# Context mean and residual input moved between the steps of a linear-attention layer

## The reference

```
x = layernorm(x + L0_attn(x))          # linear attention, 16 heads of 16
x = layernorm(x + L0_xattn(x, ctx))    # x @ W1.T + mean(ctx) @ W2.T + b
x = layernorm(x + L0_ffn(x))           # mixture of experts
```

## Time and profile before

| what | value |
|---|---|
| median of 3 runs | 2200.93 us (2196.56 to 2201.04) |
| the profiled execution | 2198.03 us, of which 2195.9 us lie between its first and last instruction |
| mean granted PE clock | 0.955 of full speed |
| PE busy, DVE busy over the span | 1986.5 us (90%), 1532.8 us (70%) |
| the attention of layer 0 | from the start to about 329 us |

### The profile page before, as it was taken

The page is one execution under the profiler, slowest core; times in us unless marked ns, Lnnn a source line. Parts: engine busy times, 40 slices in busy tenths (PEclk is TensorE's granted clock), DMA queues, the critical chain, the costliest instruction groups (busy, mean ns, idle before and its releaser), DMA issues. The chain is left out here.

```text
span 2195.9 us, 36045 instructions
## 1 busy us (share of the span) xinstructions
PE 1986.5 (90%) x12788; PEld 1413.2 (64%) x12788; DVE 1532.8 (70%) x2463; ACT 1152.0 (52%) x2215; POOL 964.9 (44%) x752
## 2 busy tenths in 40 slices
PE   7898876997988885899999999999999996799997
PEld 4565555995553553566666666666666663799996
DVE  5777764545878988588898988888888886222223
ACT  3332311110277455688877887678876772233333
POOL 2233232222322241077666666667666674222223
PEclk9999997998899997999999999999999997899998
DMA  4100007413000000200100010000000001621113
GB/s 162 40 23 23 24 16 276 171 40 113 0 0 1 1 30 0 69 1 1 31 1 1 1 40 2 1 1 1 11 1 1 1 11 68 263 74 39 36 36 127
DMA packets 37158, 95.63 MB, mean 44 GB/s; under 512 B 5492, under 2 KB 24696, under 8 KB 32248
## 3 DMA queue, kind: packets, MB, share of 16 engines
q1 hardware_dynamic: 31032, 77.07, 9.7%
q0 software_dynamic: 5952, 16.26, 2.3%
HBM read 78.89 MB, written 14.42 MB: 42 GB/s over the span
## 5 line engine op out<-in xcount | busy, mean ns | idle before, releaser
L2232 POOL TENSOR_TENSOR x_total<-x_total,x_pt 128x1024 f32<-128x1024 f32 x189 | 446.9, 2364 | 152.2 <-ACT x_pt L2318 133.5
L2341 ACT ACTIVATE x_pt<-PS,x_maskf 128x512 f32<-128x512 f32 x544 | 333.2, 689 | 125.0 <-PE PS L2677 121.3
L2445 DVE TENSOR_TENSOR PS<-x_pt,PS 128x512 f32<-128x512 f32 x480 | 333.5, 695 | 48.0 <-ACT x_pt L2341 10.5
L2463 DVE TENSOR_TENSOR x_pt<-x_pt,PS 128x1024 f32<-128x1024 f32 x320 | 323.2, 1053 | 0.7 <-PE PS L2695 0.7
L2677 PE MATMUL PS<-x_qs,x_ks 64*128 64x256 f32 x2176 | 287.9, 396 | 1.2 <-ACT x_pt L2341 1.0
L2318 ACT ACTIVATE x_pt<-x_pt 128x1536 f32<-128x1536 f32 (+1 forms) x160 | 264.1, 1664 | 13.7 <-DVE x_pt L2463 13.4
L2654 PE MATMUL PS<-x_pt,x_vs 128*64 128x256 f32 x2108 | 262.8, 388 | 2.0 <-issue 1.8
L2677 PEld LDWEIGHTS PS<-x_qs,x_ks 64*128 64x128 f32 x2176 | 195.5, 187 | 81.5 <-issue 60.1
L1163 PEld LDWEIGHTS PS<-m_xT,m_own 128*128 128x128 f32 x1984 | 236.0, 196 | 8.2 <-DVE m_own L1243 2.9
L1163 PE MATMUL PS<-m_xT,m_own 128*128 128x128 f32 x1984 | 236.9, 279 | 4.1 <-DVE m_own L1243 2.4
L1175 PE MATMUL PS<-f_w,m_hT 128*128 x992 | 224.1, 379 | 0.0
(11 more groups left out here) (321 smaller groups left out, 2914.6 us busy)
## 6 DMA issues: line engine op xcount, KB each, us to landing
f_w<-in_L_ffn_w SPq DMA_DIRECT2D x32, 1024.0 KB, 6.3
a_ctxT<-in_ctxT SPq DMA_DIRECT2D x8, 800.5 KB, 4.2
l_w<-in_ctx SPq DMA_DIRECT2D x4, 1024.0 KB
f_w<-ys SPq DMA_DIRECT2D x16, 256.0 KB, 5.2
l_w<-in_L_attn_w SPq DMA_DIRECT2D x6, 512.0 KB, 6.6
a_xT<-in_xT SPq DMA_DIRECT2D x4, 512.0 KB, 5.8
X<-in_x SPq DMA_DIRECT2D x1, 2048.0 KB, 11.2
xr<-a_xn SPq DMA_DIRECT2D x16, 128.0 KB, 1.7
```

The source lines that it names most:

```text
L2232: ins = nc.gpsimd.tensor_tensor(total2[:], first, tile[:, 2 * k + 2:2 * k + 4, :], ALU.add)
L2341: nc.scalar.activation(pt[:, s % 2, t, :].rearrange("p (h n) -> p h n", h=2), PS[:, first:first + 2, half], ACT.Identity, bias=maskf[:, b ...
L2445: ins = nc.vector.tensor_tensor(acc, tile, acc, ALU.max)
L2463: nc.vector.tensor_tensor(p_, p_, PS[:, MB, None, :].to_broadcast([P, at.stop - at.start, SPAN]), ALU.subtract).then_inc(lowered, 1)
```

## The change

- `mean(b, 0)` of batches 1 to 3 moves from place 0 of step s = 2 to the end of the step before it (1, 5, 9). `mean(b, 1)` moves from place 0 of step s = 3 to the end of the first step of the batch itself (4, 8, 12).
- The product with W2 and `context` move from the end of step s = 3 to place 1 of step s = 1 of the batch itself (1, 5, 9, 13), behind the second round of scores, and the order of the uses of the shared PSUM bank changes with them.
- `residual_input` is made for one tile in each of steps 0 to 15 (128 x 256) instead of for four tiles at once.

```diff
-            for kind, t in (("logits", g_ - 4), ("x1", g_ - 3), ("o", g_ - 2)):
+            if tile(g_ - 4):
+                OUT_USE["logits", g_ - 4] = len(OUT_USE)
+            if tile(g_) and g_ % J == 1:
+                OUT_USE["context", g_ // J] = len(OUT_USE)
+            for kind, t in (("x1", g_ - 3), ("o", g_ - 2)):
                 if tile(t):
                     OUT_USE[kind, t] = len(OUT_USE)
-            if g_ % J == J - 1 and g_ // J + 1 < B:
-                OUT_USE["context", g_ // J + 1] = len(OUT_USE)
...
-            def residual_input(b):
+            def residual_input(t):
                 pool.wait_ge(w_loaded, 16 * 7)
                 pool.wait_ge(x_loaded, 16)
-                x = X[:, b * J:(b + 1) * J, :]
-                nc.gpsimd.tensor_tensor(x, x, bout[:, None, :].to_broadcast([P, J, D]), ALU.add).then_inc(xres_ready, 1)
+                nc.gpsimd.tensor_tensor(X[:, t, :], X[:, t, :], bout[:], ALU.add).then_inc(xres_ready, 1)
...
-                if b < B and s == 3:
-                    residual_input(b)
+                if tile(g_):
+                    residual_input(g_)
...
-                dve.wait_ge(xres_ready, t // J + 1)
+                dve.wait_ge(xres_ready, t + 1)
...
+                    if place == 1 and tile(g_) and s == 1:
+                        context(g_ // J)
...
-                        if (s, place) == ((2, 0) if b else (1, 1)):
-                            mean(b, 0)
-                        if (s, place) == ((3, 0) if b else (2, 3)):
-                            mean(b, 1)
+                        if b == 0 and (s, place) in ((1, 1), (2, 3)):
+                            mean(b, s - 1)
...
-                        if b < B and s == 3:
-                            context(b)
+                        if b < B and s == 1 and b:
+                            mean(b, 0)
+                        if tile(g_) and s == 0 and g_:
+                            mean(g_ // J, 1)
...
+                if tile(g_) and s == 1:
+                    pe.wait_ge(cbc_ready, KD * b)
+                    pe.wait_ge(w_loaded, 16 * 7)
+                    product(cbc, w2t, D)
...
-                if b < B and s == 3:
-                    pe.wait_ge(cbc_ready, KD * (b + 1))
-                    pe.wait_ge(w_loaded, 16 * 7)
-                    product(cbc, w2t, D)
```

## The result

The changed kernel took 2186.66 us (median of 4 runs, 2184.01 to 2189.14), the one before 2199.41 us in the same comparison (4 runs, 2196.56 to 2201.04). The ratio is 0.994 with a 95% interval of 0.9928 to 0.9952: 13.2 us faster, between 10.6 and 15.8. The forecast was 2186.8. It hit the time more closely than it hit its terms, as the trace shows. The profiled execution of the changed kernel was the slowest of its four (2189.14 us, span 2187.0), so the spans differ by 8.9 us only.

What follows compares the result with a forecast made beforehand. PE and DVE taking turns waiting, neither full, was taken as the bound. Terms −23.4 + 4.6 + 0 + 4.6 + 0.1 = −14.1 us took the profiled 2198.03 to 2183.9, or 2186.8 on the median; range 2181.5 to 2195.

Steps and rivals of the forecast that it cites:

- The boundary: Steps 3, 7, 11: PE goes from the transposes straight into `weigh`, saving 2.14, 4.91 and 4.90 us, sum 11.95.
- the clock behind it: Steps 3, 7, 11: PE's work runs at full clock without the waits, saving 1.49, 0.55 and 2.02 us, sum 4.06.
- the means off place 0: Steps 2, 3, 6, 7, 10, 11: DVE's masks no longer come behind a mean, saving 7.1 us in all.
- mean(b, 1) at the end of steps 4, 8, 12: DVE is late for PE there; cost 1.5 us each, 4.6 with 0.1 for the small addition in step 12.
- mean(b, 0) at the end of steps 1, 5, 9: Covered by DVE's waits of 1.93 us for 2.05; cost 0, or 2.05 each without the cover.
- The context product: Place 1 of steps 1, 5, 9, 13: on PE's own path, 3 × 1.04 + 1.5 = 4.6 us cost.
- The start: Ahead of step 0 DVE drops the bias of batch 0 (0.42 us): gain 0.3 us.
- Sixteen small additions: POOL's small additions replace four large; cost is what they hold up on DVE, 0 to 9.5 us, taken as 0.1.
- the third rival: Clock falls in new places, as PE pauses at ends of steps 4, 8, 12: 7.5 us back, 2194.3; chance 0.08.
- if the clock drops elsewhere: Sign in the trace after that the forecast is wrong: a clock drop outside the stretches in steps 3, 7, 11.
- The first rival: DVE binds at the boundary, 1.3 us late three times: gain 10.2 instead of 14.1, 2190.7 us; chance 0.12.
- The last rival: The change does nothing: PE, freed of one wait, meets another at once; gain under 4.4 us; chance 0.04.

Runs made afterwards that it cites:

- changed again: The changed kernel run once more with no edit, timed against the kernel before: 2188.15 us, ratio 0.9946.
- mean in the wait: The changed kernel with mean(b, 1) of batches 1 to 3 at place 0 of steps 4, 8, 12, behind the division: 2180.52 us, ratio 0.9918.
- The halved mean: The changed kernel with mean(b, 1) of batches 1 to 3 summing only half of the 1601 columns: 2181.66 us, ratio 0.9919.
- The run with the block: The changed kernel with residual_input back as one instruction for four tiles at the end of steps -1, 3, 7, 11: 2186.97 us, ratio 0.9944.

## Why the prediction was right, and where not

The mark moved by 10.16 us, the sum said 14.1. Steps 0 to 14 became 10.5 us shorter in the first trace of the changed kernel and 12.2 in the second. By its terms, in the first:

- *The boundary, the clock behind it, the means off place 0.* Forecast for steps 2-3, 6-7, 10-11: 1.16 + 2.05 + 2.14 + 1.49 = 6.84, 0.55 + 1.4 + 4.91 + 0.55 = 7.41, 0.55 + 1.4 + 4.90 + 2.02 = 8.87. Measured 7.37, 7.55, 9.02: together 23.9 against 23.1. Right, each within 0.6 us. The experiments show the mechanism: the product alone gives 11.4 of the 13.2 us. The clock's part of this, 4.06 forecast, was read from one trace, and such dips come and go between executions (step 11 had 0.85 in the trace before, 0.92 with only `mean(b, 0)` moved), so how large this part comes out is in part luck.
- *mean(b, 1) at the end of steps 4, 8, 12.* 1.52, 1.53 and 1.53 in the trace, 4.6 forecast. Right.
- *mean(b, 0) at the end of steps 1, 5, 9.* Forecast 0. After the change DVE's mask of step 6 follows with no wait for PE and the pairs behind are as short as forecast: covered, with nothing left over. With only this mean moved step 5 took 17.62 us, against 17.63 before.
- *The context product.* Forecast 1.04, 1.04 and 1.5 for steps 5, 9, 13. Measured 2.50, 2.50 and 2.88, together 7.9 instead of 3.6. Where no dip came, step 5 took 18.49 (changed again) against 17.63 before, 0.86, and step 13 took 14.04 (mean in the wait) against 12.64, 1.40: together 0.86 + 0.86 + 1.40 = 3.1. The rest, 4.8, is the clock, which the term left out.
- *The start.* Step 2 began 1.44 us later, 0.7 was forecast. Steps 0 and 1 took 1.00 us more (30.68 against 29.68), and they take 30.67 with only the product moved and 29.68 with only the residual input, so this is the product and its bias, 1.04 in the forecast. The other 0.44 is that step 0 began later, at 45.24 instead of 44.80; it begins between 44.48 and 46.14 in the kernels of the table, and the 0.3 us forecast to be won ahead of it can't be seen in that.
- *Sixteen small additions.* Forecast 0.1. The changed kernel with either form takes the same time within 0.2 us. Right.

The step that didn't hold is the sum's term for the context product, which took the full clock for granted, on the argument in the third rival: "Against: the new pause is 1.5 us in all, the one ahead of step 11's dip was 2.92". The dip came after waits of 1.5 us (1.24 in step 13) as well, three times of three in the first trace and two of three in the second, for 1.6 us in steps 5 and 9 and 1.5 in step 13, 4.8 in all in the first trace. The rival had a chance of 0.08; on the trace it came about, at two thirds of its price of 7.5, while the gains were 0.8 larger than forecast. The halved mean and the moved one take the dips away with the pause: that the pause makes them possible is shown. Why a given one comes or not is open. The prediction had set down "if the clock drops elsewhere" as a sign that it is wrong. That sign came, and the time stayed in the range all the same.

The first rival, DVE as the bound at the boundary, had a wrong price. The forecast gave 3.9 us for a late mask of steps 4, 8 and 12. The run with the block shows the mask late and the time unchanged. The margin that I computed as 0.35 us (0.18 in the trace) guarded next to nothing; I had DVE's waits at place 0 of those steps in the trace, 3.00 us for the logits in steps 4 and 8 and 1.16 for the second scores in step 12, and didn't follow the late mask into it. The last rival, another wait for PE behind the transposes, did not come in any of the three steps.

That the total agreed within 0.2 us is thus partly luck: 14.1 was forecast for a change whose two traces show 10.5 and 12.2 in steps 0 to 14; the spans of the first pair differ by 8.9, the medians of the two comparisons by 12.7 and 12.0. Medians of before lie between 2199.4 and 2200.9, and the single runs of one kernel spread over 1.6 to 8 us.

## What to carry to other kernels

Two engines that hand work back and forth have waits on either side that hold the same loss: here the tile by tile addition gave 4.8 us alone and next to nothing once the product was moved, so parts of a change are to be priced together as well as alone. An instruction moved off a bad place still wants a wait to stand in: the same sum cost 1.5 us and risked the clock at the end of a step, and nothing inside the 3 us in which DVE waits for the logits (0.9 in step 12, where that wait is 1.16). Where an engine becomes late, follow it to its next wait before it is given a price.

## What the runs showed of the hardware

Two short waits of TensorE, 0.71 and 0.76 us with 0.44 us of work between them (changed kernel, step 5), were followed by a granted clock of 0.67 over the next 1.54 us and 0.50 (1.2 GHz) over the 1.87 behind them, in one execution of a program and not in another with the same waits. With one wait of 0.76 us (0.57 in step 13) it did not happen in three places. With only the residual input changed, a single wait of 1.90 us was followed by a low clock in step 11 and not in step 7 of the same execution.

A clip on VectorE that met an addition on GpSimd of 0.73 us instead of 2.35 us became 1.62 us shorter (2.79 to 1.17 for the pair), the whole difference.
